# Masked graph attention with f32 weighting: half of the tiles in f16 high and low parts, the subtraction shared by VectorE and GpSimd

## The chip, the cores and the metric

The kernel runs on one core of a Trainium2 chip. The time is that of the device, in microseconds. Of the kernel before there are three runs: 1684.28, 1696.18 and 1696.39 us, median 1696.18. The profile is of one more execution, which took 1695.82 us; its span on the core is 1694.0 us.

## The reference

For x (8192 x 128), ks (8192 x 128) and a 0/1 matrix adj (8192 x 8192, mostly zeros):

```
scores = einsum('nd,md->nm', x, ks)
scores = leaky_relu(scores, 0.2)
scores = where(adj > 0, scores, -9e15)
attn   = softmax(scores, axis=1)
out    = layernorm(x + einsum('nm,md->nd', attn, ks))     # eps 1e-5
```

Both products are wanted to f32 precision, and the softmax runs over 8192 columns.

## The kernel before, in words

x is cut into 32 blocks of 256 rows (`BLOCK`, two `SIDES` of 128). For one block the 8192 rows of ks are walked in 16 groups (`GROUPS`) of four tiles of 128 (`QUAD`), so there are 512 groups, and a group's work is a tile of 128 x 1024: 128 rows of ks by four times 256 rows of x. Scores are held with the rows of ks on the partitions.

Every engine has a program of its own, a loop over slots `s`, and does in a slot what the fixed delays say. Group g goes through:

- slot g, TensorE, `score` (lines 474 to 488): twelve f16 matmuls of 256 columns (high x high, high x low, low x high, for four tiles) into one of two halves of PSUM `scores`; it waits until VectorE has masked group g-2.
- slot g, ScalarE, `bend` (298): leaky relu in PSUM, scaled down by 2^-90.
- slot g, VectorE, `mask` (406): (adj <= 0) - bent, from PSUM into `ring` in SBUF, which has 24 places (`RING`); it waits for the adjacency of the group, loaded by SyncE for two groups at a time (1 MB) into a ring of four buffers (`ADJS`).
- slot g+1, VectorE, `least` (416, 419): the running minimum in PSUM. After a block's last group `columns` (425) reduces the four tiles to `col_min`.
- slot 17 of the block, TensorE, `turn` (495): transposes col_min, behind that slot's weighting. Slot 17, VectorE, `lowest` (431), behind the mask. Slot 18, TensorE, `spread` (503) brings the minimum of each row of x to all partitions, behind the scores. Slot 18, ScalarE, `spread` (308) copies it to SBUF as `floor`, behind the bend.
- slot g+19 (`AT_GAP`), GpSimd, `gap` (236): ring minus floor, 1024 elements a partition.
- slot g+21 (`AT_EXP`), ScalarE, exp in place (303), ahead of that slot's bend.
- slot g+22 (`AT_WEIGH`), TensorE, `weigh` (519), behind that slot's scores: for four tiles and two sides, the 128 x 128 probabilities in f32 times 129 columns of `k_rows` in f32 (128 of ks and one of ones, whose product is the softmax's denominator), summed in PSUM `weighted`, which has two buffers by the block's parity. The profile has two records for each of these eight f32 matmuls.
- after a block's last weighting, VectorE, `finish` (440, 445), at the end of its slot 38 of the block: reciprocal, y = weighted / denominator + x with its sum. Then the layer norm: `mean` (241) on GpSimd, `squares_of` (315) on ScalarE, `deviation` (246, 249, 251) on GpSimd, `normalise` (322) on ScalarE, each in the next slots and ahead of its engine's other work, and SyncE's `store`.
- `split_x` of the next block: high part on ScalarE (280), low part on VectorE (373), in slots 10 and 11.

Slots are numbered from a block's first group, so that slot 38 of one block is slot 22 of the next and slot 6 of the one after. What a semaphore waits for is written out by hand beside each instruction; there is no scheduler.

Before the loop ks^T and x^T are loaded into parts of the ring, their largest magnitudes give powers of two as scales (`scale_step`), and ks^T is split into f16 high and low parts (274, 367). ks by rows is loaded by SyncE as it is, behind the first adjacency loads (197). Order of VectorE in a slot: mask, lowest, least, columns, finish, split_x.

## Time and profile before

| what | value |
|---|---|
| runs | 1684.28, 1696.18, 1696.39 us |
| profiled execution | 1695.82 us, of which span 1694.0 us |
| TensorE matmuls, weight loads | busy 1624.7 us (96%), 1540.4 us (91%) |
| VectorE | busy 1344.3 us (79%) |
| ScalarE | busy 1143.1 us (67%) |
| GpSimd | busy 1240.6 us (73%) |
| mask, 512 times | 1220 ns each |
| minimum, 480 times | 1222 ns each |
| subtraction on GpSimd, 512 times | 2384 ns each |
| bend, exp, 512 times each | 1085 ns, 1047 ns |
| adjacency load, 256 times 1 MB | 4.8 us from issue to landing |
| granted clock of TensorE | 0.996 of full speed over the span |

Busy times are from the profiler's records. The ends of matmul records are modelled and neighbouring records overlap (a 256-column f16 matmul has a record of 274 ns), so TensorE's share says only that it was seldom idle; how long its work takes is read from the distance between starts. Other engines' records overlap too where one instruction directly follows another. PE in the rows is TensorE, PEld its weight loads, DVE VectorE, ACT ScalarE, POOL GpSimd, SPq SyncE's queue.

### The profile page before, as it was taken

The page shows a single profiled execution, that of the slowest core. Times are in us where ns is not written, and L with a number is a line of the kernel's source. Part 1 is how long each engine was busy: PE and PEld are TensorE (multiplying, and loading weights), DVE is VectorE, ACT ScalarE, POOL GpSimd, SP SyncE. Part 2 cuts the span into 40 slices and gives each one's busy share as a digit, 9 for nine tenths or more (in the row PEclk, how much of TensorE's full clock was granted, in tenths as well). Part 3 has the DMA queues.
Part 4 walks back from the last instruction along what each step waited for, and adds up shares of the span by engine and source line. Part 5 has one row for each costly group of instructions (what it writes and reads, how often), then busy time and mean ns, then how long its engine had stood idle before and what let it go on. Part 6 is the DMA issues. An engine that isn't in the chain of part 4 may idle for free.

```text
span 1694.0 us, 34690 instructions
## 1 busy us (share of the span) xinstructions
PE 1624.7 (96%) x14528; PEld 1540.4 (91%) x14528; DVE 1344.3 (79%) x1311; ACT 1143.1 (67%) x1297; POOL 1240.6 (73%) x650
## 2 busy tenths in 40 slices
PE   2679999999999999999999999999999999999997
PEld 1479999999999999999999999999999999999996
DVE  7988888878888888888888878887878787878860
ACT  4456767777666777766676766767676777676664
POOL 0176778787778787777877777878777878777887
PEclk9999999999999999999999999999999999999999
DMA  9734445445544554554455444445544544554410
GB/s 365 271 149 180 159 179 184 172 171 182 171 173 176 181 181 167 180 180 167 171 184 183 166 175 181 170 172 183 184 159 178 184 175 172 177 178 171 173 56 7
DMA packets 69660, 295.84 MB, mean 175 GB/s; under 512 B 6016, under 2 KB 34688, under 8 KB 36736
## 3 DMA queue, kind: packets, MB, share of 16 engines
q1 hardware_dynamic: 69504, 293.63, 49.0%
q8 instruction: 114, 1.87, 0.4%
q14 instruction: 42, 0.34, 0.1%
HBM read 289.41 MB, written 4.19 MB: 173 GB/s over the span
## 4 chain that ended last, share of the span: by engine, by line
POOL 64%; issue 33%; DMA 1%; DVE 1%; POOLq 0%; ACT 0%; SPq 0%; PE 0%; ACTq 0%; DVEq 0%
POOL ring L236 62%; POOL rstd L249 1%; DMA ring<-in_x_t 1%; POOLq L233 0%; POOL var L246 0%; POOL neg_mean L241 0%; DVE kt_lo L367 0%; SPq L169 0%; POOL shift L251 0%; SPq L172 0%; ACT kt_hi L274 0%; PE weighted L519 0%; ACT normed L322 0%; DVE ring L406 0%; DVE running L416 0%
## 5 line engine op out<-in xcount | busy, mean ns | idle before, releaser
L236 POOL TENSOR_TENSOR ring<-ring,floor 128x1024 f32<-128x1024 f32 x512 | 1200.4, 2384 | 218.8 <-ACT floor L308 218.6
L519 PE MATMUL weighted<-k_rows,ring 128*128 128x129 f32 x8192 | 999.1, 275 | 3.8 <-ACT ring L303 3.8
L519 PEld LDWEIGHTS weighted<-k_rows,ring 128*128 128x128 f32 x8192 | 955.1, 192 | 11.2 <-ACT ring L303 5.9
L298 ACT ACTIVATE scores<-scores,shrink 128x1024 f32<-128x1024 f32 x512 | 555.6, 1085 | 466.9 <-PE scores L487 466.9
L406 DVE SCALAR_TENSOR_TENSOR ring<-adj_sb,scores 128x1024 f32<-128x1024 int32 x512 | 624.4, 1220 | 287.9 <-ACT scores L298 285.3
L485 PE MATMUL scores<-xt_hi,kt_hi 128*128 128x256 f16 x2048 | 560.5, 274 | 54.2 <-DVE xt_lo L373 29.5
L419 DVE TENSOR_TENSOR running<-ring,running 128x1024 f32<-128x1024 f32 x480 | 586.5, 1222 | 0.1
L486 PE MATMUL scores<-xt_lo,kt_hi 128*128 128x256 f16 x2048 | 560.4, 274 | 0.0
L487 PE MATMUL scores<-xt_hi,kt_lo 128*128 128x256 f16 x2048 | 560.2, 274 | 0.0
L303 ACT ACTIVATE ring<-ring 128x1024 f32<-128x1024 f32 x512 | 535.8, 1047 | 16.2 <-POOL ring L236 16.2
L485 PEld LDWEIGHTS scores<-xt_hi,kt_hi 128*128 128x128 f16 x2048 | 201.6, 98 | 77.5 <-DVE ring L406 29.9
L486 PEld LDWEIGHTS scores<-xt_lo,kt_hi 128*128 128x128 f16 x2048 | 201.1, 98 | 24.3
L487 PEld LDWEIGHTS scores<-xt_hi,kt_lo 128*128 128x128 f16 x2048 | 201.2, 98 | 24.0
L241 POOL TENSOR_SCALAR neg_mean<-y_sum 128x2 f32<-128x2 f32 x32 | 6.2, 193 | 196.4 <-DVE y L445 196.3
L373 DVE SCALAR_TENSOR_TENSOR xt_lo<-xt_raw,scale,xt_hi 128x256 f16<-128x256 f32 x32 | 49.9, 1558 | 0.3 <-ACT xt_hi L280 0.3
L322 ACT ACTIVATE normed<-y,shift,rstd 128x128 f32<-128x128 f32 x64 | 28.1, 486 | 25.1 <-POOL shift L251 25.1
L425 DVE TENSOR_REDUCE col_min<-running 128x256 f32<-128x1024 f32 x32 | 39.2, 1224 | 1.1
L416 DVE COPY running<-ring 128x1024 f32<-128x1024 f32 x32 | 39.0, 1217 | 0.0
L440 DVE RECIPROCAL recip<-weighted 128x2 f32<-128x2 f32 x32 | 5.3, 165 | 42.4 <-PE weighted L519 42.4
L315 ACT ACTIVATE squares<-y,neg_mean 128x128 bf16<-128x128 f32 x64 | 25.7, 401 | 18.4 <-POOL neg_mean L241 17.3
L249 POOL TENSOR_TENSOR rstd<-var,minus_half 128x2 f32<-128x2 f32 x32 | 22.5, 703 | 2.7
L445 DVE SCALAR_TENSOR_TENSOR y<-weighted,recip,x_row 128x128 f32<-128x128 f32 x64 | 19.9, 348 | 3.2
(34 smaller groups left out, 171.6 us busy)
## 6 DMA issues: line engine op xcount, KB each, us to landing
adj_sb<-in_adj SPq DMA_DIRECT2D x256, 1024.0 KB, 4.8
ring<-in_ks_t SPq DMA_DIRECT2D x8, 512.0 KB, 6.5
ring<-in_x_t SPq DMA_DIRECT2D x8, 512.0 KB, 12.8
xt_raw<-in_x_t SPq DMA_DIRECT2D x32, 128.0 KB, 4.8
k_rows<-in_ks SPq DMA_DIRECT2D x8, 512.0 KB, 7.4
x_row<-in_x SPq DMA_DIRECT2D x32, 128.0 KB, 4.8
out<-normed SPq DMA_DIRECT2D x32, 128.0 KB, 5.1
```

What stands on the lines that cost most here:

```text
L236: nc.gpsimd.tensor_tensor(here, here, below, ALU.subtract).then_inc(gap_ready, 1)
L249: nc.gpsimd.tensor_tensor(rstd[:, :], var[:, :], minus_half[:, :], ALU.pow).then_inc(rstd_ready, 1)
L298: nc.scalar.activation(here, here, ACT.Prelu, scale=shrink[:, :], alpha=SLOPE).then_inc(bent_ready, 1)
L303: nc.scalar.activation(here, here, ACT.Exp, scale=-(2.0 ** SHRINK)).then_inc(prob_ready, 1)
L373: nc.vector.scalar_tensor_tensor(xt_lo[:, b % 2, :], xt_raw[:, b % 2, :], scale_x, xt_hi[:, b % 2, :], ALU.mult, ALU.subtract).then_inc(xt ...
L406: nc.vector.scalar_tensor_tensor(ring[:, g % RING, :, :], adj_sb[:, n % ADJS, half * QUAD:(half + 1) * QUAD, :], 0.0, scores[:, g % 2, :, ...
L419: nc.vector.tensor_tensor(running[:, :, :], here, running[:, :, :], ALU.min)\
L425: nc.vector.tensor_reduce(col_min[:, :], running[:, :, :].rearrange("p t n -> p n t"), AX.X, ALU.min)\
L485: nc.tensor.matmul(to, kt_hi[:, cols], xt_hi[:, at, :], start=True, stop=False)
L486: nc.tensor.matmul(to, kt_hi[:, cols], xt_lo[:, at, :], start=False, stop=False)
L487: last = nc.tensor.matmul(to, kt_lo[:, cols], xt_hi[:, at, :], start=False, stop=True)
L519: last = nc.tensor.matmul(weighted[:, b % 2, j * LANES:(j + 1) * LANES], ring[:, g % RING, t, j * P:(j + 1) * P], k_rows[:, rows, 0:LANES] ...
```

## The change

Of the four tiles of a group two (`WHOLE`) are weighted in f32 as before. For the other two (`PARTED`) the probabilities are cut into f16 high and low parts, and so are the rows of ks; the products high x high, high x low and low x high are summed, the second without the column of ones. The exp gets a bias (`PROB_LIFT`, 14 powers of two). ScalarE makes the high part (slot g+22, ahead of the exp), GpSimd the low part (slot g+22, behind the subtraction), into three buffers; the weighting moves to slot g+23. The subtraction is now done by VectorE for the first one (even groups) or two tiles (odd groups), reading the spread minimum in PSUM `floors`, and by GpSimd for the other three or two.

For that, PSUM is divided anew: `weighted` has one buffer, `floors` two halves of a bank, and the transposed col_min goes into `running`. `finish` moves from the end of VectorE's slot 38 to the front of its slot 39 and gets a step `denom`. The adjacency ring has 3 buffers instead of 4. The rows of ks are scaled on the chip now, so their loads wait for the scales; half of them lands in the ring's places 18 to 21 (`ks_raw`), ScalarE makes its high part in slot 6, GpSimd scales both halves and makes the low part ahead of its loop.

```diff
-    ADJS = 4
+    ADJS = 3
+    WHOLE = 2
+    PARTED = QUAD - WHOLE
+    PARTS = 3
-    AT_GAP, AT_EXP, AT_WEIGH = 19, 21, 22
+    AT_GAP, AT_EXP, AT_PART, AT_WEIGH = 19, 21, 22, 23
...
-        weighted = ps("weighted", [P, 2, 512], F32)
+        weighted = ps("weighted", [P, 512], F32)
+        floors = ps("floors", [P, 2, BLOCK], F32)
...
+        def dve_tiles(g):
+            return 1 + g % 2
...
# SyncE, ahead of its loop
-            for c in range(STEPS):
-                rows = slice(c * TILES // STEPS, (c + 1) * TILES // STEPS)
-                sp.dma_start(k_rows[:, rows, 0:D], ks[:, rows, :]).then_inc(k_rows_loaded[c], 16)
+            sp.wait_ge(scale_step, SCALE_STEPS)
+            for j in range(GROUPS):
+                sp.dma_start(k_rows[:, j, :, 0:D], ks_v[:, j, 0:WHOLE, :]).then_inc(k_rows_loaded, 16)
+            sp.dma_start(ks_raw.rearrange("p (j t) d -> p j t d", t=PARTED), ks_v[:, :, WHOLE:QUAD, :])\
+                .then_inc(ks_raw_loaded, 16)
...
# GpSimd
+            def part_rows():
+                pool.wait_ge(scale_step, SCALE_STEPS)
+                pool.wait_ge(k_hi_ready, 1)
...
+                nc.gpsimd.tensor_scalar(ks_raw, ks_raw, scale_k, 1.0, ALU.mult, ALU.mult).then_inc(k_scaled_ready, 1)
+                pool.wait_ge(k_rows_loaded, 16 * GROUPS)
+                nc.gpsimd.tensor_scalar(k_rows[:, :, :, 0:D], k_rows[:, :, :, 0:D], scale_k, 1.0, ALU.mult, ALU.mult)\
+                    .then_inc(k_rows_ready, 1)
+                pool.wait_ge(k_scaled_ready, 1)
+                nc.gpsimd.tensor_tensor(low, ks_raw, high, ALU.subtract).then_inc(k_lo_ready, 1)
...
             def gap(g):
+                first = dve_tiles(g)
...
-                here = ring[:, g % RING, :, :]
-                below = floor[:, b % 2, :].unsqueeze(1).to_broadcast([P, QUAD, BLOCK])
+                here = ring[:, g % RING, first:, :]
+                below = floor[:, b % 2, :].unsqueeze(1).to_broadcast([P, QUAD - first, BLOCK])
                 nc.gpsimd.tensor_tensor(here, here, below, ALU.subtract).then_inc(gap_ready, 1)
+
+            def low_part(g):
+                pool.wait_ge(part_hi_ready, g + 1)
+                nc.gpsimd.tensor_tensor(pt_lo[:, g % PARTS, :, :], ring[:, g % RING, WHOLE:, :],
+                                        pt_hi[:, g % PARTS, :, :], ALU.subtract).then_inc(part_lo_ready, 1)
...
# ScalarE
-                nc.scalar.activation(here, here, ACT.Exp, scale=-(2.0 ** SHRINK)).then_inc(prob_ready, 1)
+                nc.scalar.activation(here, here, ACT.Exp, bias=lift[:, :], scale=-(2.0 ** SHRINK))\
+                    .then_inc(prob_ready, 1)
+
+            def high_part(g):
+                act.wait_ge(prob_ready, g + 1)
+                wait(act, weighted_ready, g + 1 - PARTS)
+                nc.scalar.activation(pt_hi[:, g % PARTS, :, :], ring[:, g % RING, WHOLE:, :], ACT.Copy)\
+                    .then_inc(part_hi_ready, 1)
...
# VectorE
+            def gap(g):
+                b, j = divmod(g, GROUPS)
+                tiles = dve_tiles(g)
+                dve.wait_ge(spread_ready, b + 1)
+                if j == LAST and b + 1 < BLOCKS:
+                    dve.wait_ge(floor_ready, b + 2)
+                else:
+                    dve.wait_ge(floor_ready, b + 1)
+                dve.wait_ge(running_ready, g + 1)
+                here = ring[:, g % RING, 0:tiles, :]
+                below = floors[:, b % 2:b % 2 + 1, :].to_broadcast([P, tiles, BLOCK])
+                nc.vector.tensor_tensor(here, here, below, ALU.subtract).then_inc(dve_gap_ready, 1)
...
             def finish(b):
...
+                nc.vector.tensor_scalar(denom[:, :], total[:, :, ONES], scale_k, None, ALU.mult).then_inc(denom_ready, 1)
+                dve.wait_ge(denom_ready, b + 1)
                 wait(dve, y_ready, SIDES * b)
-                nc.vector.reciprocal(recip[:, :], total[:, :, ONES]).then_inc(recip_ready, 1)
+                nc.vector.reciprocal(recip[:, :], denom[:, :]).then_inc(recip_ready, 1)
...
             for s in SLOTS:
+                b = whole(s, AT_FINISH)
+                if b is not None:
+                    finish(b)
                 g = group(s, 0)
                 if g is not None:
                     mask(g)
                 b = whole(s, AT_SPREAD - 1)
                 if b is not None:
                     lowest(b)
+                g = group(s, AT_GAP)
+                if g is not None:
+                    gap(g)
                 g = group(s, 1)
                 if g is not None:
                     least(g)
                     if g % GROUPS == LAST:
                         columns(g // GROUPS)
-                b = whole(s, AT_FINISH)
-                if b is not None:
-                    finish(b)
...
# TensorE, in weigh
                 if q == 0:
-                    pe.wait_ge(floor_ready, b + 1)
...
+                    wait(pe, y_ready, SIDES * b)
...
+                for t in range(WHOLE):
                     for j in range(SIDES):
-                        first = rows == 0 and j == 0
-                        last = nc.tensor.matmul(weighted[:, b % 2, j * LANES:(j + 1) * LANES],
-                                                ring[:, g % RING, t, j * P:(j + 1) * P], k_rows[:, rows, 0:LANES],
-                                                start=first, stop=(rows == TILES - 1), skip_group_check=True)
+                        nc.tensor.matmul(weighted[:, j * LANES:(j + 1) * LANES],
+                                         ring[:, g % RING, t, j * P:(j + 1) * P], k_rows[:, q, t, 0:LANES],
+                                         start=(q == t == j == 0), stop=False, skip_group_check=True)
+                pe.wait_ge(part_hi_ready, g + 1)
+                pe.wait_ge(part_lo_ready, g + 1)
+                for t in range(PARTED):
...
+                        nc.tensor.matmul(weighted[:, at:at + LANES], pt_hi[:, g % PARTS, t, cols], high,
+                                         start=False, stop=False, skip_group_check=True)
+                        nc.tensor.matmul(weighted[:, at:at + D], pt_hi[:, g % PARTS, t, cols], low,
+                                         start=False, stop=False, skip_group_check=True)
+                        last = nc.tensor.matmul(weighted[:, at:at + LANES], pt_lo[:, g % PARTS, t, cols], high,
+                                                start=False, stop=done, skip_group_check=True)
```

## Rows read from the trace of the kernel before

**Rows 1.** Busy time of each engine, from the page.

```profile
PE 1624.7 (96%) x14528; PEld 1540.4 (91%) x14528; DVE 1344.3 (79%) x1311; ACT 1143.1 (67%) x1297; POOL 1240.6 (73%) x650
```

**Rows 2.** Chain of waits: start us, us, what; two of 31 alike.

```profile
863.66 23.50 POOL ring L236 x10
...
914.05 23.51 POOL ring L236 x10
```

**Rows 3.** Timeline, GpSimd, the layer norm's small steps.

```profile
910.52 0.19 POOL L246 TENSOR_SCALAR var<-square_sum 128x2 f32<-128x2 f32 x1
...
911.73 9.35 POOL L236 TENSOR_TENSOR ring<-ring,floor 128x1024 f32<-128x1024 f32 x4
```

**Rows 4.** Timeline, TensorE in one slot: start us, us, engine, operation.

```profile
905.01 0.10 PEld L485 LDWEIGHTS scores<-xt_hi,kt_hi 128*128 128x128 f16 x1
905.12 0.27 PE L485 MATMUL scores<-xt_hi,kt_hi 128*128 128x256 f16 x1
...
906.32 1.87 PEld L519 LDWEIGHTS weighted<-k_rows,ring 128*128 128x128 f32 x16
...
908.11 0.10 PEld L485 LDWEIGHTS scores<-xt_hi,kt_hi 128*128 128x128 f16 x1
```

**Rows 5.** Waits, 907.39 to 957.78 us: waiter, releaser, us, times, longest.

```profile
DVE ring L406 <- ACT scores L298: 9.3, 12, 1.2
```

**Rows 6.** Timeline, the tail: last subtractions and last weighting.

```profile
1645.24 9.34 POOL L236 TENSOR_TENSOR ring<-ring,floor 128x1024 f32<-128x1024 f32 x4 [2.37 <-ACT floor L308]
...
1685.15 2.05 PE L519 MATMUL weighted<-k_rows,ring 128*128 128x129 f32 x16 [0.27 <-ACT ring L303]
```

**Rows 7.** Timeline, the slots before and around finish.

```profile
903.33 1.95 PE L519 MATMUL weighted<-k_rows,ring 128*128 128x129 f32 x16
...
904.65 1.22 DVE L406 SCALAR_TENSOR_TENSOR ring<-adj_sb,scores 128x1024 f32<-128x1024 int32 x1 [0.74 <-ACT scores L298]
...
905.79 1.22 DVE L419 TENSOR_TENSOR running<-ring,running 128x1024 f32<-128x1024 f32 x1
...
906.92 0.16 DVE L440 RECIPROCAL recip<-weighted 128x2 f32<-128x2 f32 x1
907.19 0.35 DVE L445 SCALAR_TENSOR_TENSOR y<-weighted,recip,x_row 128x128 f32<-128x128 f32 x1
...
907.75 1.22 DVE L406 SCALAR_TENSOR_TENSOR ring<-adj_sb,scores 128x1024 f32<-128x1024 int32 x1
```

**Rows 8.** Groups by line: busy us, mean ns of one | idle before.

```profile
L425 DVE TENSOR_REDUCE col_min<-running 128x256 f32<-128x1024 f32 x32 | 39.2, 1224 | 1.1
...
L431 DVE TENSOR_REDUCE low<-weighted 128x2 f32<-128x256 f32 x32 | 13.4, 418 | 0.5 <-PE weighted L495 0.5
L308 ACT ACTIVATE floor<-weighted 128x256 f32<-128x256 f32 x32 | 12.1, 377 | 3.9 <-PE weighted L503 3.9
```

**Rows 9.** The instructions of line 373: ns min/median/max.

```profile
L373 DVE SCALAR_TENSOR_TENSOR xt_lo<-xt_raw,scale,xt_hi x32: 478/1273/11595, 28.9 to 1577.5; 128x256 f16<-128x256 f32 x32
```

**Rows 10.** Timeline, ScalarE, the layer norm's steps.

```profile
908.13 0.40 ACT L315 ACTIVATE squares<-y,neg_mean 128x128 bf16<-128x128 f32 x1 [0.41 <-POOL neg_mean L241]
...
909.06 1.04 ACT L303 ACTIVATE ring<-ring 128x1024 f32<-128x1024 f32 x1
910.00 1.07 ACT L298 ACTIVATE scores<-scores,shrink 128x1024 f32<-128x1024 f32 x1
911.80 0.88 ACT L322 ACTIVATE normed<-y,shift,rstd 128x128 f32<-128x128 f32 x2 [0.73 <-POOL shift L251]
```

**Rows 11.** Timeline, the start: SyncE's queue, and the last scale step.

```profile
16.98 26.21 SPq L197 DMA_DIRECT2D k_rows<-in_ks  x8
...
28.36 0.21 DVE L393 TENSOR_SCALAR shrink<-unscale 128x1 f32<-128x1 f32 x1
```

**Rows 12.** Timeline, TensorE after the longest wait of the run.

```profile
75.35 0.69 PE L495 MATMUL weighted<-eye,col_min 128*128 128x128 f32 x2 [3.17 <-DVE col_min L425]
75.83 0.42 PE L485 MATMUL scores<-xt_hi,kt_hi 128*128 128x256 f16 x1
```

More of the change, by code:

```diff
@@ L105, in adj_attention_layernorm @@
         running = ps("running", [P, QUAD, BLOCK], F32)
-        weighted = ps("weighted", [P, 2, 512], F32)
+        weighted = ps("weighted", [P, 512], F32)
+        floors = ps("floors", [P, 2, BLOCK], F32)
         ks_t_loaded = [sem(f"ks_t_loaded{c}") for c in range(STEPS)]
         x_t_loaded = [sem(f"x_t_loaded{c}") for c in range(STEPS)]
-        k_rows_loaded = [sem(f"k_rows_loaded{c}") for c in range(STEPS)]
+        k_rows_loaded = sem("k_rows_loaded")
+        ks_raw_loaded = sem("ks_raw_loaded")
+        k_rows_ready = sem("k_rows_ready")
+        k_hi_ready = sem("k_hi_ready")
+        k_scaled_ready = sem("k_scaled_ready")
+        k_lo_ready = sem("k_lo_ready")
         adj_loaded = [sem(f"adj_loaded{j}") for j in range(ADJS)]
@@ L262, in _ @@
                     gap(g)
+                g = group(s, AT_PART)
+                if g is not None:
+                    low_part(g)
         @block.scalar
@@ L307, in spread @@
                 wait(act, gap_ready, GROUPS * (b - 1))
-                nc.scalar.activation(floor[:, b % 2, :], weighted[:, b % 2, 256:256 + BLOCK], ACT.Copy)\
+                nc.scalar.activation(floor[:, b % 2, :], floors[:, b % 2, :], ACT.Copy)\
                     .then_inc(floor_ready, 1)
@@ L331, in _ @@
                     normalise(b)
+                g = group(s, AT_PART)
+                if g is not None:
+                    high_part(g)
                 g = group(s, AT_EXP)
@@ L414, in least @@
                 if g % GROUPS == 0:
-                    wait(dve, col_min_ready, g // GROUPS)
+                    wait(dve, low_ready, g // GROUPS)
                     nc.vector.tensor_copy(running[:, :, :], here).then_inc(running_ready, 1)
@@ L457, in _ @@
                     lowest(b)
+                g = group(s, AT_GAP)
+                if g is not None:
+                    gap(g)
                 g = group(s, 1)
@@ L492, in turn @@
                 pe.wait_ge(col_min_ready, b + 1)
-                wait(pe, y_ready, SIDES * (b - 1))
                 for j in range(SIDES):
-                    last = nc.tensor.transpose(weighted[:, b % 2, j * P:(j + 1) * P], col_min[:, j * P:(j + 1) * P],
+                    last = nc.tensor.transpose(running[:, 0, j * P:(j + 1) * P], col_min[:, j * P:(j + 1) * P],
                                                eye[:, :])
@@ L501, in spread @@
                 pe.wait_ge(low_ready, b + 1)
+                wait(pe, floor_ready, b)
+                wait(pe, dve_gap_ready, GROUPS * b - 1)
                 for j in range(SIDES):
-                    last = nc.tensor.matmul(weighted[:, b % 2, 256 + j * P:256 + (j + 1) * P],
+                    last = nc.tensor.matmul(floors[:, b % 2, j * P:(j + 1) * P],
                                             low[:, b % 2, j:j + 1].to_broadcast([P, P]), eye[:, :],
```

52 lines of the change are left out of this document (42 added, 10 removed).

## The prediction, made before the changed kernel was run

> **What bounds the kernel now.** I read the busy times first: TensorE is matmul-busy for 96% of the span, VectorE 79%, GpSimd 73%, ScalarE 67% [rows 1]. The chain of waits then shows the repetition: 31 runs of ten GpSimd subtractions, 50.39 us apart in the steady part [rows 2], which is the period of a block of 16 groups. That GpSimd heads this chain is no proof that it sets the pace: ten subtractions take 23.50 us, so one takes 2.35 us and sixteen with the 1.2 us of layer-norm steps [rows 3] take 38.8 of 50.4 us. The timeline settles it. TensorE's weight loads go from one group's first score to the next group's without a gap: 3.10 us, of which 1.31 us are the scores (to the first load of the weighting) and 1.79 us the weighting [rows 4]. 16 x 3.10 is 49.6; the other 0.8 us are the transposes and the spread. VectorE instead waits 9.3 us a period for ScalarE's bend, which waits for scores [rows 5]. TensorE's own work sets the pace, with nothing of the other engines on the path until the tail, where 16 subtractions at 2.35 us follow the last floor [rows 6].
>
> **The change, step by step.** I number slots as the kernel does, the first group of a block in its slot 0; slot 38 is the last weighting of that block.
>
> *TensorE.* Half of the 16 records of f32 weighting stay: 0.895 us. Twelve f16 matmuls of 128 or 129 columns come. The trace has f16 matmuls of 256 columns, 0.11 us apart (1.31/12 = 0.109) [rows 4]; scaled with the columns one takes 0.056 us, which is the lower end. The upper end is a weight load that can't be hidden by such a short matmul: its record has 0.10 us. I take 0.056, because the f32 loads (1.87 us for sixteen, one every 0.112, so the last lasts 0.19) overlap one another in the records [rows 4], so a record's length isn't the engine's pace. Weighting: 0.895 + 0.67 = 1.57 us; slot 2.88 instead of 3.10; TensorE's own work in a period 46.9 us. The Trainium skill (TensorE: Matmul & The Clock Gate, Back-to-back issue gap) speaks against this: it gives about 81 ns for each matmul of 128 columns in a stream of load and matmul pairs. By it the weighting would be 1.87 us, longer than before, and the time about 1815 us. No stream of that width is in this trace.
>
> *VectorE.* The mask follows the end of the scores by 1.32 us (903.33, where the weighting starts, to 904.65); then mask 1.14 to the minimum, minimum 1.13 to the next, the finish 0.83 [rows 7]. So records overlap by 0.09. A subtraction is new. Of 256 elements it has the row of the reduction that makes low (418 ns); 1024 elements take 1.22; by the line between them 512 take 0.69 [rows 7, 8]. Less the overlap: 0.33 and 0.60 us. The finish gets one more small dependent step, as reciprocal to y: 0.27 us [rows 7], so 1.10, and 1.15 until TensorE sees it. Sum over a period: 16 x 2.27 + 16 x 0.465 + 1.19 for xt_lo [rows 9] + 1.14 for the columns + 0.33 + 1.10 = 47.5 us.
>
> *GpSimd.* 2.35 us at 1024 elements and about 0.2 for a tiny one give 1.27 at 512 and 1.81 at 768 [rows 2, 3]: the subtraction 1.54 on average, the low part 1.27, so 2.81 a slot and 46.2 us with the small steps. f16 operands on GpSimd are in no row: not less than the 1.27, at most twice. With about 2.4 us waiting for the squares in slot 41 it has 48.6: near, but not first.
>
> *ScalarE.* The high part is a copy of 512: between 377 ns at 256 and 1.04 us at 1024 [rows 8, 10], 0.60, less overlap 0.52. Exp 0.95, bend 1.01, squares 0.93, normalise 0.79 [rows 10]. An ordinary slot is 2.48 us, under the slot of every other engine.
>
> **What is late next** decides more than the sums. `weighted` has one buffer now, so the first weighting of a block (slot 39) waits for y, and y comes from VectorE after all of slot 38. From the end of slot 38's scores: 1.32 + 1.14 + 0.60 + 1.13 + 1.15 = 5.34 us to y. TensorE is there after 2.88. It waits 2.46 us, and all scores behind it too. Before, this wait wasn't there. The second is the turn: TensorE waits in slot 49 for the column minima, which VectorE makes at the end of slot 48. I follow one turn of the cycle:
> - y to mask of slot 40: weighting 1.57, scores 1.31, bend 1.32: 4.20 us, VectorE partly idle.
> - That mask to the column minima: nine masks and minima 20.43, five subtractions of 0.60 and four of 0.33, 4.32, xt_lo 1.19, columns 1.24 with the signal: 27.18.
> - ScalarE holds up VectorE twice there. Slot 41: squares 0.93 + high 0.52 + exp 0.95 + bend 1.12 = 3.52 against VectorE's 2.87. Slot 42: normalise 0.79 + 0.52 + 0.95 + 1.01 = 3.27 against 2.60. Together 1.32.
> - Turn, spread, five scores and four weightings to the end of the scores of the next slot 38: 0.9 + 6.55 + 6.28 = 13.73.
> - The 5.34 again.
>
> Sum: 51.8 us, 1.4 more than 50.4, though TensorE has 2.7 us less work. The 2.46 us and some 2.2 us of waits at the turn take it back.
>
> *Other edits.* The adjacency ring of 3: a load of 1 MB is needed every two slots, 5.8 us, and takes 4.8 us to land (table above), and three buffers put it some four slots ahead; cost 0, and where that cover is short, as in the start, the masks wait for it. Start: the loads of ks rows wait for the last scale step, whose instruction runs at 28.36 us, where they were issued from 16.98 on and held SyncE's queue for 26.2 us [rows 11]; the adjacency loads behind them come late by what the shift leaves over; ScalarE's copy of 4096 elements in slot 6 (eight of the 512 slopes, 3.6 us) delays one mask. GpSimd's three passes of 4096 (at most 8.8 us each by its slope) end before slot 18. I take +4, between 0 and +15. Tail: after the last floor at 1645.24 the span had 48.8 us [rows 6]: 37.6 of subtractions, 1.4 small steps, 9.8 from the last one's end. Now 16 x 2.81 + 1.4 + three low parts more, 3.8, + 9.8 = 60: +11.
>
> Total: 30.5 periods x 1.4 = +43, +4, +11, so 1752 us of span from 1694.0, and with the 1.8 us around it 1754. The profiled execution (1695.82) stands 0.4 under the median, so I say 1755.
>
> **The rivals.**
> 1. *Only the capacities count*: the two waits are absorbed. Then VectorE bounds with 47.5: 1696 - 2.9 x 30.5 + 15 = 1623 us, faster. For it: before, no engine's coupling cost anything. Against: y can't be ready before mask, minimum and finish of slot 38. It turns faster by 1% where TensorE's waits stay under 2.4 us a period in all, for its work is 46.9. Chance 0.13.
> 2. *Only the y wait remains*, the turn is met in time: 46.9 + 2.5 to 50.4, so 1680 to 1711. Chance 0.12.
> 3. *Weight loads set the f16 pace*, up to 0.098 us each: slot 3.38, 54.9 us in a period, y wait 5.34 - 3.38 = 1.96: 56.9, so 1696 + 6.5 x 30.5 + 15 = 1909; half way 1830. For it: nothing so narrow in f16 is shown. Against: the overlapping f32 loads. Chance 0.12.
> 4. *The clock falls in the waits.* After the 3.17 us wait in the first block matmuls ran at 0.42 instead of 0.27 us [rows 12], 1.2 instead of 2.4 GHz. If one slot's 2.88 us runs so after each wait, 1.4 us are lost, twice a period: +85, 1840. My waits are shorter than that one. Chance 0.07.
> 5. *GpSimd bounds*: the low part 25% dearer makes 3.13 a slot, 53.8 a period, 1815. Chance 0.06.
>
> Forecast 0.5, as 1712 to 1800. That the f16 weighting isn't done at all I exclude from the diff.
>
> **How the numbers follow.** Within 1% (some 1679 to 1713, about what a measurement here can tell from no change) lies rival 2: 0.13 with the edges. Faster: rival 1, 0.14. Slower: the rest, 0.73. The range leaves out rival 1 and the far end of rivals 3 and 5: 1672 to 1845.
>
> **What would show it.** TensorE waiting about 2.5 us for y before one weighting per block and about 2 us for col_min; f16 weighting matmuls 0.056 us apart; a period of 51.8; VectorE 47.5 busy less overlaps; the subtraction at 418 and 690 ns; GpSimd at 1.3 us a low part. It is wrong if the period is under 50 (rival 1) or if TensorE has no waits yet a slot over 3.1 (rival 3).

## The result, and the profile after

| kernel | runs | median | span of the profiled run |
|---|---|---|---|
| before | 4 | 1695.55 us (1684.28 to 1696.39) | 1694.0 us |
| changed | 4 | 1757.85 us (1755.99 to 1761.13) | 1755.0 us |

The ratio is 1.0383, with a 95% interval of 1.0353 to 1.0414: slower. The forecast was 1755 us. One of the four runs of the kernel before is more than 10 us shorter than the other three, and no trace shows why.

The first part of the page, as [rows 1]: TensorE is busy less, every other engine more, and no engine is near 100%.

```profile
PE 1554.2 (89%) x16576; PEld 1446.4 (82%) x16576; DVE 1547.7 (88%) x1855; ACT 1441.9 (82%) x1810; POOL 1408.3 (80%) x1167
```

The finish steps stand 50.39 or 50.40 us apart in the kernel before; in the changed kernel 19 of the 29 steady periods are 51.8 us long (one of them 52.0) and ten are 53.3 to 53.5 us. The profile's stretches of two such periods that follow one another (busy time of the engines with counts, granted clock, share of the DMA engines, GB/s) show what sets them apart, the clock of TensorE, with the same 518 records:

```profile
199.36:251.16 51.80, 47.55 (x518) 44.66 (x518) 47.50 (x58) 44.36 (x57) 43.51 (x36) 1.00 0.49 171
251.16:304.52 53.36, 49.20 (x518) 45.77 (x518) 47.51 (x58) 44.37 (x57) 43.51 (x36) 0.97 0.48 166
```

The waits in one of the shorter periods, as [rows 5]:

```profile
DVE ring L479 <- ACT scores L351: 4.1, 6, 1.8
POOL var L295 <- ACT squares L381: 2.8, 1, 2.8
...
PE weighted L611 <- DVE y L534: 2.4, 1, 2.4
...
PE running L586 <- DVE col_min L498: 1.7, 1, 1.7
```

TensorE waits 2.4 us for y and 1.7 us for the column minima, both once in the period. The timeline of TensorE around the wait for y, as [rows 4]:

```profile
931.05 0.27 PE L579 MATMUL scores<-xt_hi,kt_lo 128*128 128x256 f16 x1
933.75 1.13 PE L611 MATMUL weighted<-k_rows,ring 128*128 128x129 f32 x8 [2.42 <-DVE y L534]
934.72 0.22 PE L623 MATMUL weighted<-k_parts,pt_hi 128*128 128x129 f16 x1
934.77 0.22 PE L625 MATMUL weighted<-k_parts,pt_hi 128*128 128x128 f16 x1
```

and its weight loads there:

```profile
934.72 0.10 PEld L625 LDWEIGHTS weighted<-k_parts,pt_hi 128*128 128x128 f16 x1
934.77 0.10 PEld L627 LDWEIGHTS weighted<-k_parts,pt_lo 128*128 128x128 f16 x1
```

The f16 matmuls of the weighting start 0.056 us apart and so do their loads, though each load's record has 0.10 us. From 933.75 to 935.40, where the next scores begin, the weighting takes 1.65 us after the wait; in an undisturbed slot it is 1.57. A wait's number understates what it costs: it is counted from the modelled end of the matmul before, while the starts, 0.11 us apart otherwise, are 2.70 us apart here (931.05 to 933.75). By starts TensorE loses 2.6 us at y, and 0.08 more in the weighting behind it.

VectorE over the whole cycle, as [rows 7], from the mask of slot 38 to the next finish:

```profile
929.59 1.22 DVE L479 SCALAR_TENSOR_TENSOR ring<-adj_sb,scores 128x1024 f32<-128x1024 int32 x1 [0.19 <-ACT scores L351]
...
932.46 0.21 DVE L526 TENSOR_SCALAR denom<-weighted,scale 128x2 f32<-128x2 f32 x1
...
938.03 1.22 DVE L479 SCALAR_TENSOR_TENSOR ring<-adj_sb,scores 128x1024 f32<-128x1024 int32 x1 [1.82 <-ACT scores L351]
...
964.85 1.23 DVE L498 TENSOR_REDUCE col_min<-running 128x256 f32<-128x1024 f32 x1
...
984.27 0.21 DVE L526 TENSOR_SCALAR denom<-weighted,scale 128x2 f32<-128x2 f32 x1
```

and the two places of TensorE that close it, the transposes of the turn and the end of slot 54's scores, where the weighting starts:

```profile
966.13 0.44 PE L586 MATMUL running<-eye,col_min 128*128 128x128 f32 x2 [1.70 <-DVE col_min L498]
...
980.08 1.06 PE L611 MATMUL weighted<-k_rows,ring 128*128 128x129 f32 x8
```

The groups of instructions that are new or of a new size, as [rows 8]:

```profile
L284 POOL TENSOR_TENSOR pt_lo<-ring,pt_hi 128x512 f16<-128x512 f32 x512 | 594.4, 1162 | 13.1 <-ACT pt_hi L363 13.1
...
L280 POOL TENSOR_TENSOR ring<-ring,floor 128x768 f32<-128x768 f32 x256 | 471.3, 1841 | 100.9 <-ACT floor L374 100.9
...
L280 POOL TENSOR_TENSOR ring<-ring,floor 128x512 f32<-128x512 f32 x256 | 326.3, 1275 | 0.0
...
L513 DVE TENSOR_TENSOR ring<-ring,floors 128x512 f32<-128x512 f32 x256 | 173.4, 677 | 1.5 <-PE floors L596 1.5
L513 DVE TENSOR_TENSOR ring<-ring,floors 128x256 f32<-128x256 f32 x256 | 105.2, 411 | 0.0
```

### The profile page after: what moved, and what is told of

Its sections match the earlier page's. It is cut to its first block and busy times, and to the rows that moved or that the text cites. A ratio compares the mean times of both kernels' runs of the same rounds, so it can differ in the third digit from the quotient of the medians.

```text
span 1755.0 us, 42403 instructions
## 1 busy us (share of the span) xinstructions
PE 1554.2 (89%) x16576; PEld 1446.4 (82%) x16576; DVE 1547.7 (88%) x1855; ACT 1441.9 (82%) x1810; POOL 1408.3 (80%) x1167
## 5 line engine op out<-in xcount | busy, mean ns | idle before, releaser
L280 POOL TENSOR_TENSOR ring<-ring,floor 128x768 f32<-128x768 f32 (+1 forms) x512 | 797.5, 1558 | 100.9 <-ACT floor L374 100.9
L611 PE MATMUL weighted<-k_rows,ring 128*128 128x129 f32 x4096 | 547.8, 277 | 74.3 <-DVE y L534 74.3
L284 POOL TENSOR_TENSOR pt_lo<-ring,pt_hi 128x512 f16<-128x512 f32 x512 | 594.4, 1162 | 13.1 <-ACT pt_hi L363 13.1
L357 ACT ACTIVATE ring<-ring,lift 128x1024 f32<-128x1024 f32 x512 | 583.9, 1140 | 1.3 <-DVE ring L513 0.7
L611 PEld LDWEIGHTS weighted<-k_rows,ring 128*128 128x128 f32 x4096 | 501.0, 192 | 87.1 <-issue 80.5
L623 PE MATMUL weighted<-k_parts,pt_hi 128*128 128x129 f16 x2048 | 378.4, 220 | 10.9 <-POOL pt_lo L284 10.9
L627 PE MATMUL weighted<-k_parts,pt_lo 128*128 128x129 f16 x2048 | 380.1, 223 | 0.0
L625 PE MATMUL weighted<-k_parts,pt_hi 128*128 128x128 f16 x2048 | 378.6, 220 | 0.0
L363 ACT ACTIVATE pt_hi<-ring 128x512 f16<-128x512 f32 x512 | 318.9, 623 | 8.8 <-PE weighted L627 8.3
L623 PEld LDWEIGHTS weighted<-k_parts,pt_hi 128*128 128x128 f16 x2048 | 202.8, 99 | 13.1 <-issue 8.4
L625 PEld LDWEIGHTS weighted<-k_parts,pt_hi 128*128 128x128 f16 x2048 | 199.6, 97 | 6.4
```

What stands on the lines that cost most here:

```text
L280: nc.gpsimd.tensor_tensor(here, here, below, ALU.subtract).then_inc(gap_ready, 1)
L284: nc.gpsimd.tensor_tensor(pt_lo[:, g % PARTS, :, :], ring[:, g % RING, WHOLE:, :], pt_hi[:, g % PARTS, :, :], ALU.subtract).then_inc(part_ ...
L357: nc.scalar.activation(here, here, ACT.Exp, bias=lift[:, :], scale=-(2.0 ** SHRINK))\
L611: nc.tensor.matmul(weighted[:, j * LANES:(j + 1) * LANES], ring[:, g % RING, t, j * P:(j + 1) * P], k_rows[:, q, t, 0:LANES], start=(q == ...
L623: nc.tensor.matmul(weighted[:, at:at + LANES], pt_hi[:, g % PARTS, t, cols], high, start=False, stop=False, skip_group_check=True)
L625: nc.tensor.matmul(weighted[:, at:at + D], pt_hi[:, g % PARTS, t, cols], low, start=False, stop=False, skip_group_check=True)
```

## Where the 61 us came from

| stretch | before | changed | difference |
|---|---|---|---|
| start to the first finish | 151.0 us | 145.9 us | -5.1 |
| 29 periods, waits: 29 x (51.80 - 50.40) | | | +40.7 |
| 29 periods, clock: the ten long ones | | | +16.0 |
| from there to the end | 81.5 us | 91.0 us | +9.4 |

That is +61.0, the difference of the spans.

## The experiments

Each has four runs, and was compared with runs of the kernel before on its own chip; the eleven kernels were run on three chips in all, on which the kernel before had medians of 1696.1, 1695.6 and 1695.1 us. The period is the distance between two finishes.

| kernel | time | ratio to before (95%) | period |
|---|---|---|---|
| changed | 1757.9 | 1.038 (1.035 to 1.041) | 51.8, 10 of 29 at 53.4 |
| finish early | 1687.8 | 0.995 (0.994 to 0.997) | 50.1 |
| one tile | 1736.7 | 1.024 (1.022 to 1.026) | 50.7, 10 at 52.3 to 52.4 |
| all on GpSimd | 1916.3 | 1.129 (1.127 to 1.131) | 56.7 |
| before, one buffer | 1923.0 | 1.134 (1.132 to 1.136) | 58.0 |
| before, wait for y as changed | 1743.2 | 1.029 (1.027 to 1.030) | 52.0 |
| scores ahead | 1722.9 | 1.017 (1.014 to 1.020) | 50.9, 7 at 52.1 to 52.2 |
| filled wait | 1741.1 | 1.027 (1.025 to 1.028) | 51.8 |
| minimum in SBUF | 1813.3 | 1.070 (1.067 to 1.074) | 52.5, 21 at 53.7 to 54.8 |
| catch up | 1667.5 | 0.985 (0.981 to 0.988) | 49.2 |
| four edits | 1620.3 | 0.957 (0.954 to 0.959) | 48.2 |
| turn behind | 1582.3 | 0.933 (0.932 to 0.935) | 47.0 |

### Is the wait for y on the path?

**Finish early.**

```diff
             for s in SLOTS:
-                b = whole(s, AT_FINISH)
-                if b is not None:
-                    finish(b)
                 g = group(s, 0)
                 if g is not None:
                     mask(g)
+                b = whole(s, AT_FINISH - 1)
+                if b is not None:
+                    finish(b)
```

> The changed kernel (period 51.8 us, 1757.9 us) with one edit: VectorE's finish stands behind the mask of slot 38 instead of at the front of slot 39. My theory, that the wait for y is on the path: y comes 0.60 (subtraction) + 1.13 (minimum) = 1.7 us earlier, TensorE waits about 0.7 us for y instead of 2.4, all of it is won, the period is about 50.1 us and the time about 1705 us. Rival (VectorE's or GpSimd's own work bounds): the wait for y shrinks, another grows by as much, the time stays within 1% of 1758.

Measured: 1687.8 us and a period of 50.08, where 50.1 was forecast. The waits of TensorE in one period:

```profile
PE running L586 <- DVE col_min L498: 1.7, 1, 1.7
...
PE weighted L611 <- DVE y L534: 0.7, 1, 0.7
```

The wait for y fell from 2.4 to 0.7 us and TensorE's other wait did not grow. The time is 17 us better than forecast, because I had left the clock out: no period of this kernel is longer than 50.24, so the 16 us of the clock went too. The rival, that the bound is an engine's own work, falls: the edit takes no work away.

**Before, one buffer.** The same wait put into the kernel before, with nothing else of the change:

```diff
-                wait(pe, y_ready, SIDES * (b - 1))
...
                 if q == 0:
-                    pe.wait_ge(floor_ready, b + 1)
+                    wait(pe, y_ready, SIDES * b)
...
-                        last = nc.tensor.matmul(weighted[:, b % 2, j * LANES:(j + 1) * LANES],
+                        last = nc.tensor.matmul(weighted[:, 0, j * LANES:(j + 1) * LANES],
```

> The kernel before with one edit: the weighted sum has one PSUM buffer, so a block's first weighting waits for y of the block before; the other bank takes the transposes and the spread. All weighting stays f32, no work is moved. My theory: from the end of the scores to y are 1.32 + 1.14 + 1.13 + 0.83 + 0.1 = 4.5 us by the trace of before, TensorE is there after 3.10: it waits 1.4 us a block, all lost, period 51.8, 1696 + 31 x 1.4 = 1740 us. Rival (the wait is absorbed elsewhere, the loss of the change comes from its other parts): within 1% of 1696 us.

Measured: 1923.0 us, period 58.0, far off. The expectation had a slot wrong: in the kernel before, the first weighting of a block stands in slot 38, the slot at whose end finish stands, and not in slot 39, so TensorE meets the wait at the end of the scores and sits through all of the 4.5 us. The timeline of TensorE (start us, us, operation, and in brackets the idle time ahead and its releaser) shows the second half of the loss:

```profile
962.15 3.78 PE L520 MATMUL weighted<-k_rows,ring 128*128 128x129 f32 x16 [4.47 <-DVE y L445]
```

These sixteen f32 records take 3.78 us instead of 1.95 [rows 7]: TensorE's granted clock is 0.5 there, 1.2 GHz, for 6.8 us that begin in the last microsecond of the wait, and falls so in every period. 4.5 us of waiting and 3.1 more behind it make the 7.6 us.

**Before, wait for y as changed.** The same, with the slots of the changed kernel:

```diff
-    AT_GAP, AT_EXP, AT_WEIGH = 19, 21, 22
+    AT_GAP, AT_EXP, AT_WEIGH = 19, 21, 23
...
             for s in SLOTS:
+                b = whole(s, AT_FINISH)
+                if b is not None:
+                    finish(b)
                 g = group(s, 0)
...
-                b = whole(s, AT_FINISH)
-                if b is not None:
-                    finish(b)
```

> The kernel before with one PSUM buffer for the weighted sum, and now with the weighting in slot g+23 and finish at the front of slot 39, as the changed kernel has them; all weighting in f32 and all subtraction on GpSimd. In the first try the weighting stood one slot earlier, so that y was late by 4.5 us and not by 1.4. Theory: y comes 1.32 + 1.14 + 1.13 + 0.83 + 0.1 = 4.5 us after the end of slot 38's scores, TensorE is there after 3.10, waits 1.4 us a block, the clock stays at full, the period is 51.8 us: 1696 + 29 x 1.4 + 3 for the slot more = 1740 us. Rival (the wait is absorbed): 1696 to 1700 us.

Measured: 1743.2 us, period 52.0.

```profile
PE weighted L520 <- DVE y L445: 1.4, 1, 1.4
```

The wait is 1.4 us as worked out, is lost whole, and the clock stays. The period is 0.2 us longer than 50.4 + 1.4, and the starts of TensorE's instructions show why: the last matmul of the scores starts at 929.64 us and the weighting at 931.28, 1.64 apart where it is 0.11 otherwise, and the weighting has 0.07 us more than in another slot. That is 1.60 us, the whole of 52.0 - 50.4; the wait as printed leaves out what the matmul's record overlaps. So a kernel with all weighting in f32 and no new work loses 48 us to this wait alone.

### Why are some periods 1.6 us longer?

In the changed kernel the timeline of TensorE at a period that is long (start us, us, operation) reads:

```profile
252.45 1.13 PE L611 MATMUL weighted<-k_rows,ring 128*128 128x129 f32 x8 [2.43 <-DVE y L534]
...
254.37 0.42 PE L577 MATMUL scores<-xt_hi,kt_hi 128*128 128x256 f16 x1
254.58 0.42 PE L578 MATMUL scores<-xt_lo,kt_hi 128*128 128x256 f16 x1
```

Behind the 2.4 us wait the first weighting starts at full speed; 1.9 us after its start the matmuls of 256 columns have 0.42 us records, 0.21 apart, and by the profile's stretches of one microsecond the granted clock is 0.9 at 253, 0.5 from 254 to 257 and 0.9 at 257. In all ten long periods the clock falls 0.8 to 1.5 us after the start of this weighting, and in none at the turn.

**Scores ahead.** No work added or removed, only TensorE's order in slot 39:

```diff
-                if g is not None:
+                if g is not None and g not in ahead:
                     score(g)
...
+                b = whole(s, AT_WEIGH)
+                if b is not None and b > 0 and group(s + 1, 0) is not None:
+                    score(s + 1)
+                    ahead.add(s + 1)
                 g = group(s, AT_WEIGH)
                 if g is not None:
                     weigh(g)
```

> The changed kernel with one edit on TensorE: in slot 39 the scores of slot 40 are made before the first weighting of the new block, so TensorE has 1.31 us of work while it waits for y. No work is added or taken away. My theory: the wait for y falls from 2.4 to 1.1 us, the period of 51.8 us by 1.3 to 50.5, and the clock no longer falls in a third of the periods (10 of 29, 1.6 us each = 16 us): 1758 - 1.3 x 30 - 16 = 1703 us. If the fall of the clock has another cause than this wait (the turn's wait, 1.7 us), some periods are still 1.6 us longer: 1719 us. Rival (VectorE or GpSimd bounds): the wait moves to another place, 1740 us or more.

Measured: 1722.9 us. Two periods, one without and one with a fall of the clock, and the waits in the second:

```profile
349.67:400.54 50.87, 47.61 (x520) 44.71 (x518) 48.32 (x59) 44.63 (x57) 43.56 (x36) 1.00 0.49 174
400.54:452.69 52.15, 49.02 (x520) 45.83 (x518) 48.31 (x59) 44.62 (x57) 43.55 (x36) 0.97 0.47 170
```

```profile
PE running L586 <- DVE col_min L498: 2.0, 1, 2.0
...
PE weighted L611 <- DVE y L534: 1.1, 1, 1.1
```

The wait for y is 1.1 us as forecast, but 7 of 29 periods are still long, and there the clock falls at 433 us, right at the turn, whose wait has grown from 1.7 to 2.0 us; it is the turn in all seven. So the wait for y isn't the only one that can do it. The ordinary period is 0.9 shorter, not 1.3: VectorE is busy 48.3 instead of 47.5 us, since xt_lo now takes 1.56 us on average and not 0.73. It has two inputs in SBUF. It starts early in a subtraction of GpSimd now (at 826.25 us, GpSimd's ends at 827.53 and xt_lo at 827.82), where in the changed kernel it starts late in a low part (at 845.27, GpSimd's ends at 845.65 and xt_lo at 845.94).

**Filled wait.** The same scores made once more in the wait, as added work that signals nothing:

```diff
+                b = whole(s, AT_WEIGH)
+                if b is not None and b > 0 and group(s + 1, 0) is not None:
+                    score(s + 1, signal=False)
```

> The changed kernel with work added to TensorE: ahead of each block's first weighting, where it waits for y, it makes the scores of the next slot once without signalling them (they are made again in their own slot), 1.31 us a block. Theory (the clock falls because of the idle wait for y): TensorE is busy for half of that wait, the clock stays, no period is longer than 51.8 us, and the kernel with more work is faster by 16 us: 1742 us. Rival A (the wait at the turn, 1.7 us, makes the clock fall, as it does in the kernel with scores ahead, where it is 2.0 us): as before, 1758 us. Rival B (added work costs its time): 1758 + 31 x 1.3 = 1798 us.

Measured: 1741.1 us; all 29 periods lie between 51.80 and 51.97. TensorE's waits over the whole run, 31 or 32 of each:

```profile
PE running L587 <- DVE col_min L498: 55.9, 32, 3.2
...
PE weighted L612 <- DVE y L534: 35.1, 31, 1.3
```

The turn's wait is what it was in the changed kernel (1.7 us), the wait for y is 1.1 us with work in front, and no period is long: in the changed kernel it was the 2.4 us of idleness before y that let the clock fall. 1.31 us more work in each block made the kernel 17 us faster. The kernels here, by TensorE's longest wait in a steady period: at 2.0 us (scores ahead) 7 of 29 periods lose the clock, at 2.2 (one tile) and 2.4 (changed) 10 each, at 3.0 (minimum in SBUF, below) 21, at 4.5 (before, one buffer) all 29, and with no wait above 1.9 us none.

### Who makes the turn's wait, and how near is GpSimd?

**One tile.** `return 1 + g % 2` becomes `return 1` in `dve_tiles`.

> The changed kernel with VectorE subtracting one tile of every group (256 elements a partition) and GpSimd three, instead of 1.5 and 2.5. My theory: VectorE is 0.27 us shorter in the odd slots, of which slot 38 (wait for y) and the five from 40 to 48 (wait at the turn) are on the path: 6 x 0.27 = 1.6 us, period about 50.2, if GpSimd, with 16 x (1.80 + 1.12) + 1.2 = 47.9 and the 2.8 us it waits for the squares, 50.7, doesn't come first; so 50.2 to 50.8 and 1710 to 1727 us plus about 4 in the tail. Rival, GpSimd is the bound already: slower by 8 x 0.53 = 4.2 us a period, about 1890 us.

Measured: 1736.7 us.

```profile
203.56:255.90 52.34, 49.34 (x518) 46.28 (x518) 45.42 (x59) 44.42 (x57) 47.75 (x37) 0.97 0.49 169
255.90:306.61 50.71, 47.72 (x518) 44.74 (x518) 45.41 (x59) 44.42 (x57) 47.75 (x37) 1.00 0.51 175
```

The ordinary period is 50.71 us, the figure that GpSimd's work and wait gave, and not the 50.2 that VectorE's relief alone would give; the turn's wait fell from 1.7 to 0.7 us. The time is above my 1727 because 10 periods still have the clock's fall, 16 us, behind the 2.2 us that are left before y; I had forgotten it again. The first finish is also 5.3 us later than in the changed kernel; the xt_lo ahead of it took 7.49 us and not 1.50. In the period GpSimd waits only for the squares (2.2 us) and for y (0.6): it is the next in line.

**All on GpSimd.** `dve_tiles` returns 0, VectorE's subtraction and the waits for it go.

> The changed kernel with the whole subtraction back on GpSimd, VectorE does none. My theory: GpSimd has 2.35 + 1.12 = 3.47 us a slot, 55.5 in a period, with 1.2 of small steps and up to 2.8 waiting for the squares 56.7 to 59.5: slower than the changed kernel by 5 to 8 us a period, 1910 to 2010 us. VectorE's waits grow. Rival (the loss of the change is VectorE's new instruction, GpSimd has room): faster than 1758, towards 1700 us.

Measured: 1916.3 us, period 56.75, at the lower end of what 3.47 us a slot gave.

```profile
PE weighted L618 <- POOL pt_lo L284: 6.3, 13, 1.7
```

TensorE waits for GpSimd's low part in 13 weightings of the period: GpSimd bounds. Given the low parts, the sharing of the subtraction is worth 158 us, so it isn't what made the changed kernel slow.

**Minimum in SBUF.** VectorE reads `floor`; `floors` goes and `weighted` has two buffers again:

```diff
-        weighted = ps("weighted", [P, 512], F32)
-        floors = ps("floors", [P, 2, BLOCK], F32)
+        weighted = ps("weighted", [P, 2, 512], F32)
...
-                below = floors[:, b % 2:b % 2 + 1, :].to_broadcast([P, tiles, BLOCK])
+                below = floor[:, b % 2:b % 2 + 1, :].to_broadcast([P, tiles, BLOCK])
...
-                    wait(pe, y_ready, SIDES * b)
+                    pe.wait_ge(floor_ready, b + 1)
```

> The changed kernel with VectorE reading the minimum in SBUF (floor, the copy that GpSimd reads) instead of PSUM. That frees a PSUM bank: the weighted sum has two buffers again and no weighting waits for y. VectorE's subtraction then has both inputs in SBUF. Theory A (the PSUM operand is what keeps VectorE out of GpSimd's way): xt_lo, which has two SBUF inputs, took 0.48 us alone and 1.27 us beside GpSimd; if each subtraction grows by as much as 0.8 us VectorE gets 16 x 0.8 = 13 us more and the period is about 58 us, 1950 us. Theory B (there is little contention): no wait for y, no clock loss, period 48 to 49.5 us, 1650 to 1690 us.

Measured: 1813.3 us, between the two theories. Its groups:

```profile
L283 POOL TENSOR_TENSOR pt_lo<-ring,pt_hi 128x512 f16<-128x512 f32 x512 | 692.6, 1353 | 8.2 <-ACT pt_hi L362 7.8
...
L510 DVE TENSOR_TENSOR ring<-ring,floor 128x512 f32<-128x512 f32 x256 | 286.0, 1117 | 0.0
...
L510 DVE TENSOR_TENSOR ring<-ring,floor 128x256 f32<-128x256 f32 x256 | 162.2, 634 | 0.0
```

VectorE's subtraction takes 1117 and 634 ns where it took 677 and 411, 5.3 us more in a period, and GpSimd's instructions grow as well, the low part from 1162 to 1353 ns. The wait for y is gone and the kernel is slower by 55 us. Not all of that is the subtraction itself: VectorE comes later to the turn, and TensorE's wait there is 3.0 us, behind which the clock falls in 21 of the 29 periods.

```profile
PE running L583 <- DVE col_min L498: 3.0, 1, 3.0
```

The records of the 512 subtractions tell a block from a slowdown. 207 of them take 408 to 417 or 675 to 717 ns, about as in the changed kernel; the other 305 take up to 2.3 us, and each of these ends a fixed time after the end of an instruction of GpSimd, 0.28 us at 256 elements and 0.55 us at 512. So VectorE's instruction is held until one of GpSimd's has ended, and from there it needs the same time in each case. The Trainium skill (SBUF — State Buffer, Who interferes with whom) says that a VectorE instruction with two SBUF inputs contends with a GpSimd instruction that reads SBUF, and of VectorE's modes with two ports that whoever comes first keeps the shared ports for its whole instruction; the 305 records agree with that here too. The two engines get in each other's way when both of VectorE's inputs lie in SBUF; with this order of steps the PSUM bank for the minimum is well spent, and the single `weighted` buffer is its price.

### A version that keeps the change and loses the waits

**Catch up.** Finish early, and in `dve_tiles`:

```diff
-            return 1 + g % 2
+            return 1 if 5 <= g % GROUPS <= 13 else 1 + g % 2
```

> The kernel with finish behind the mask of slot 38 (1687.8 us, period 50.08) with one more edit: VectorE subtracts one tile only in slots 40 to 48, where it is behind, and 1 or 2 elsewhere as before. Theory (the wait at the turn, 1.75 us, comes from VectorE's backlog): VectorE is 5 x 0.27 = 1.35 us shorter there, the period is 48.7 us, if GpSimd, with 45.9 us of work and up to 2.8 us waiting for the squares, allows it (48.7 as well): 1645 to 1650 us. Rival (GpSimd or ScalarE comes first): no change, 1688 us, or slower.

Measured: 1667.5 us, period 49.2.

```profile
PE running L586 <- DVE col_min L498: 0.7, 1, 0.7
PE weighted L611 <- DVE y L534: 0.7, 1, 0.7
```

The turn's wait is 0.7 instead of 1.7 us: it was VectorE's backlog. Of the 1.35 us taken from VectorE the period got 0.85 shorter. Read from starts, TensorE's own 47.0 us, 0.93 lost at y, 0.86 at the turn, 0.30 before the spread and 0.12 for one low part sum to 49.2, the whole period.

**Four edits.** Finish early, catch up, scores ahead, and `return 3` for the groups of the last block.

> The edits of the previous kernel (finish behind the mask of slot 38, one tile in slots 40 to 48) with the scores of slot 40 ahead of the first weighting, and VectorE subtracting three of four tiles in the last block, where it is idle. Theory: period between 47.6 (TensorE's 46.9 and what is left of the turn's wait) and 48.7 us (GpSimd); in the tail GpSimd has 0.7 + 1.12 us a group instead of 2.7, 13 us less: 1605 to 1637 us. If GpSimd already bounds the period, only the tail is won against the kernel without these two edits.

Measured: 1620.3 us, period 48.20. No wait for y is left. From the last but two finishes to the end are 78.4 us instead of 95.2.

**Turn behind.** TensorE's order at the turn:

```diff
-                b = whole(s, AT_SPREAD)
-                if b is not None:
-                    spread(b)
                 b = whole(s, AT_WEIGH)
...
+                b = whole(s, AT_SPREAD)
+                if b is not None:
+                    spread(b)
                 b = whole(s, AT_TURN)
                 if b is not None:
+                    if group(s + 1, 0) is not None:
+                        score(s + 1)
+                        ahead.add(s + 1)
                     turn(b)
```

> The kernel with four edits (1620.3 us, period 48.20) with TensorE's order at the turn changed as it was at y: the scores of slot 50 are made ahead of the transposes of col_min, and the spread stands behind slot 50's weighting instead of ahead of it. Theory: the 0.7 us of waiting at the turn and the 0.4 us before the spread go, period 47.1 to 47.5 us, 1588 to 1600 us. Rival (GpSimd, 91% busy, or VectorE, 93%, comes first): the wait moves, 1610 to 1625 us.

Measured: 1582.3 us, 6.7% under the kernel before, period 46.97. The busy times over the span, and all waits in one period that sum to 0.5 us or more (the third number is the longest single one):

```profile
PE 1515.6 (96%) x16576; PEld 1433.0 (91%) x16576; DVE 1503.0 (95%) x1855; ACT 1437.5 (91%) x1810; POOL 1478.3 (94%) x1167
```

```profile
ACT scores L353 <- PE scores L581: 1.5, 7, 0.2
ACT floor L376 <- PE floors L598: 1.2, 1, 1.2
DVE ring L481 <- ACT scores L353: 0.9, 3, 0.4
POOL var L297 <- ACT squares L383: 0.5, 1, 0.5
```

No wait of TensorE is among them, and 46.97 is TensorE's own work as the prediction summed it (46.9). It is a little better than my 47.1 to 47.5, and 6 us under the 1588 us forecast. So TensorE's own work bounds again, as in the kernel before, with 3.4 us less of it in a period (46.97 against 50.39). This kernel has every part of the change; only the order of four steps and the split of the subtraction differ.

## Why the prediction was right

- **The f16 pace.** Taken as 0.056 us from columns, between 0.056 and 0.098; measured 0.056. The loads' records of 0.10 us start every 0.056 us, so the argument from the overlapping f32 loads held. The 81 ns that the Trainium skill gives for a 128-column stream (TensorE: Matmul & The Clock Gate, Back-to-back issue gap) is not what this stream does, and rival 3 falls.
- **VectorE.** The subtraction was taken at 418 and 690 ns and has 411 and 677; the finish with its new step was taken at 1.10 us to the next mask and has 1.06; the period's busy sum 47.5 by forecast and 47.5 by the profile. Two errors are hidden in it: xt_lo had 0.67 us and not 1.27, and where a wait follows, records don't overlap, which I had subtracted everywhere.
- **GpSimd.** Low part 1162 ns instead of 1270 in f16, the subtraction 1275 and 1841; waits for the squares 2.8 instead of 2.4 us. Near, not first: right, and the one-tile kernel shows how near.
- **ScalarE.** The copy was taken at 0.60 us and has 0.623. The exp was left at its old price and grew from 1047 to 1140 ns; no wait of TensorE in the period above ends on it.
- **The ring of three.** Taken at 0, and no mask of the changed kernel waits for a load.
- **The cycle.** Its legs, forecast and measured: y to the mask of slot 40, 4.20 and 4.31 (933.72 to 938.03); to the turn, 27.18 + 1.32 = 28.50 and 28.10 (to 966.13), with VectorE held up by ScalarE 0.50 and 0.64 us in slots 41 and 42 where I had 1.32 together; to the end of slot 54's scores 13.73 and 13.95 (to 980.08); to y 5.34 and 5.45. Sum 51.8 and 51.81. The waits in it: 2.46 us forecast at y and 2.42 measured; some 2.2 at the turn and 1.7 measured, or by starts 1.9 and 0.3 more before the spread. One number beside it is a slip: TensorE has not 2.7 us less work in a period but 3.5 by the prediction's own figures (16 x 0.22), 3.4 measured; the sum doesn't use it.
- **The clock.** Rival 4, given 0.07, happened beside the forecast, not in its place: in a third of the periods, always at the wait for y, 1.6 us each. The prediction's reason against it, that its waits are shorter than the 3.17 us of [rows 12], was too weak. 16 us were missing from the sum.
- **Start.** Forecast +4, measured -5.1, and the reason isn't in the prediction. GpSimd's three passes end at 66.2 us (below), and the first subtraction starts at 83.34 us, 3.4 us later than before, as forecast. But from there to the first finish the changed kernel needs 62.5 us and the one before 71.0, because the kernel before stands still once in this stretch: its xt_lo at 105.80 us takes 11.60 us, the maximum in the row of which the prediction took the median [rows 9]. It sits through five subtractions of GpSimd and ends 0.28 us after the last one before a pause, at 117.12. TensorE is idle 8.23 us for the mask behind it, and its granted clock is 1.2 GHz from 115.7 to 122.5 us. By starts TensorE loses 10.3 us: 8.4 in that wait, and 1.2 and 0.7 in the scores and the weighting behind it. In the changed kernel the same instruction takes 1.50 us. Without that stop the kernel before would have its first finish at about 140.7 us (an estimate, 151.0 - 10.3), the changed one has it 5.2 us later, near the forecast +4. So the 9 us here are a term that the prediction didn't have. Which kernel meets the stop is in the runs: with the whole subtraction on GpSimd this xt_lo takes 10.7 to 14.0 us (four kernels), with three of four tiles there 7.49, and with the changed kernel's sharing or a later version of it 0.5 to 1.5.
- **Tail.** Forecast +11, measured +9.4.

The stop in the kernel before (GpSimd, VectorE, TensorE), and VectorE's instruction in the changed kernel:

```profile
103.22 13.90 POOL L236 TENSOR_TENSOR ring<-ring,floor 128x1024 f32<-128x1024 f32 x6
...
105.80 11.60 DVE L373 SCALAR_TENSOR_TENSOR xt_lo<-xt_raw,scale,xt_hi 128x256 f16<-128x256 f32 x1
...
118.58 0.40 PE L485 MATMUL scores<-xt_hi,kt_hi 128*128 128x256 f16 x1 [8.23 <-DVE ring L406]
```

```profile
109.86 1.50 DVE L444 SCALAR_TENSOR_TENSOR xt_lo<-xt_raw,scale,xt_hi 128x256 f16<-128x256 f32 x1
```

GpSimd at the start of the changed kernel, the first and the last of the three passes and the first subtractions:

```profile
51.20 3.68 POOL L265 TENSOR_SCALAR ring<-ring,scale 128x4096 f32<-128x4096 f32 x1 [23.18 <-ACT k_parts L368]
...
58.54 7.66 POOL L270 TENSOR_TENSOR k_parts<-ring,k_parts 128x4096 f16<-128x4096 f32 x1
...
83.34 6.03 POOL L280 TENSOR_TENSOR ring<-ring,floor 128x768 f32<-128x768 f32 x4 [17.14 <-ACT floor L374]
```

The passes over 4096 elements with one input take 3.7 us and the one with two inputs 7.66, under the 8.8 us that I had as a bound.

So that the median came out 3 us from the forecast is luck: the terms that were off (the clock +16 missing, the start 9 too high, 1.5 periods' loss and the tail 4 too high) nearly cancel. The sign, and the size of a period, are not luck: the legs of the cycle were each right to 0.4 us, and the two waits that close it are shown by the edits that remove them.

## What to carry to other kernels

Where a change takes a buffer away, look for the wait that this makes and work out when its releaser comes: here 3.4 us less work for TensorE a block became 1.4 us more time, and the order of a few steps with the split of the subtraction decided between 1758 and 1582 us. Walk the cycle through all engines from one such wait back to itself; the busy sums alone (47.5 here) gave neither the sign nor the size. An engine that waits can have its wait filled by moving its own next work in front of it, which adds no work; look then which wait grows, since the clock fell at the turn once its wait had gone from 1.7 to 2.0 us. And read a row's maximum beside its median: one instruction of 11.60 us in the kernel before moved the start by 10 us.

## What the runs showed of the hardware that I had not expected

- TensorE's clock falls to 1.2 GHz behind waits of 2.0 to 3.0 us in some periods (7 of 29 at 2.0, 10 at 2.2, 10 at 2.4, 21 at 3.0) and behind 4.5 us in all; with waits up to 1.9 us it never fell in the steady part. Filling half of a wait with useless matmuls made the kernel 1% faster.
- VectorE with both inputs in SBUF beside a busy GpSimd: a subtraction of 512 elements 1117 instead of 677 ns, one of 256 elements 634 instead of 411, and GpSimd's low part 16% longer, all on average. With one input in PSUM the 512 subtractions stay within 404 to 421 and 672 to 686 ns.
- VectorE is blocked there, not slowed down, until an instruction of GpSimd ends. The 256-element xt_lo takes 0.48 us undisturbed; in 31 of 32 cases of the changed kernel and 30 of 32 of the one before it takes longer, and it always ends 0.28 us after an instruction of GpSimd. It doesn't always get its turn at the first such end: in the kernel before it once stood through five subtractions in a row, 11.60 us.
- GpSimd's tensor-tensor with an f16 input and output is not slower but faster than in f32: 1162 against 1275 ns for 512 elements. With one input it does 4096 elements in 3.7 us, 0.9 ns each.
